# Reordered steps around the routing of an attention and mixture-of-experts block, with the residual kept divided by its gate and written into one of the two accumulators

## The reference

```
sa, ca, ga, sb, cb, gb = (silu(c) @ wmod) in six parts
ga, gb = sign * max(|g|, 0.25)
h = layernorm(x) * (1 + ca) + sa
r = h + recurrent_attention(h)
x = x + ga * (r + (silu(h2 @ Wgate) * (h2 @ Wval)) @ Wout)       # h2 = layernorm(r)
h = layernorm(x) * (1 + cb) + sb                                 # (2*512, 256)
p = softmax(h @ gate_weight.T)                                   # 16 experts, top 4 of each token
y = sum over the 4 of p_e * down_e(silu(gate_e h) * up_e h)      # 176 hidden
  + down_s(silu(gate_s h) * up_s h)                              # shared expert, 352 hidden
out = x + gb * y
```

## Time and profile before

| | |
|---|---|
| time, median of 3 runs | 368.24 us (368.22 to 368.97) |
| the profiled execution's own time | 365.12 us |
| its span, first to last instruction | 363.3 us |
| mean granted TensorE clock | 0.948 of full speed |
| PE busy | 317.4 us (87%) |
| DVE busy | 209.1 us (58%) |
| ACT busy | 176.0 us (48%) |
| POOL busy | 162.8 us (45%) |
| chain that ended last | PE 67%, DVE 15%, ACT 5%, DMA 5%, issue 4% |

### The profile page before, as it was taken

One profiled execution on the slowest core, in us unless ns is written; L12 is line 12 of the kernel. 1 busy time (PEld: TensorE's weight loads), 2 busy tenths in 40 slices (PEclk: granted clock), 3 DMA queues, 4 the chain that ended last, 5 costly groups with the idle time before them and its releaser, 6 DMA issues.

```text
span 363.3 us, 5639 instructions
## 1 busy us (share of the span) xinstructions
PE 317.4 (87%) x1424; PEld 236.1 (65%) x1424; DVE 209.1 (58%) x607; ACT 176.0 (48%) x338; POOL 162.8 (45%) x156
## 2 busy tenths in 40 slices
PE   6998989999999997999699787999999999999500
PEld 3785555766678876877497565777777777777300
DVE  4778998589576546594558834344343343343146
ACT  3488986798883533553271212443443444444200
POOL 3364487910001003256355571466566566666510
PEclk9889999999999999999988989999999999999855
DMA  6911031100019772002899464577766767765483
GB/s 206 359 68 59 1 115 59 60 0 0 2 48 361 158 144 73 2 17 98 231 321 325 150 204 157 111 111 108 121 113 105 115 118 109 120 113 62 56 231 133
DMA packets 43993, 44.91 MB, mean 124 GB/s; under 512 B 3387, under 2 KB 39995, under 8 KB 43963
## 3 DMA queue, kind: packets, MB, share of 16 engines
q1 hardware_dynamic: 35659, 33.66, 32.5%
q0 software_dynamic: 8304, 10.88, 18.7%
HBM read 27.74 MB, written 16.79 MB: 123 GB/s over the span
## 4 chain that ended last, share of the span: by engine, by line
PE 67%; DVE 15%; ACT 5%; DMA 5%; issue 4%; POOL 1%; SPq 1%; DVEq 0%; ACTq 0%; POOLq 0%
PE ps L1773 15%; PE ps L1800 10%; PE ps L1599 3%; PE ps L1361 3%; PE ps L1604 3%; PE ps L1600 3%; PE ps L1378 3%; PE ps L1362 3%; PE ps L1759 3%; PE ps L1786 3%; DMA acc_rows<-w,ids 2%; PE ps L1411 2%; PE ps L1418 1%; DVE w L1341 1%; DMA w<-in_wmod 1%
## 5 line engine op out<-in xcount | busy, mean ns | idle before, releaser
L546 POOL DMA_INDIRECT acc_rows<-w,ids x47 | 73.4, 1562 | 52.2 <-ACT w L866 49.6
L1773 PE MATMUL ps<-wup,w 128*128 x188 | 63.6, 460 | 1.5 <-DVE hm L1287 1.4
L1313 DVE TENSOR_TENSOR sg<-sg,ps 128x176 f32<-128x176 f32 x47 | 15.9, 338 | 68.4 <-ACT sg L858 68.4
L1800 PE MATMUL ps<-wdown,w 88*128 x188 | 48.6, 380 | 0.6 <-DVE w L1321 0.6
L533 POOL DMA_INDIRECT xs_rows<-h3x,slots x32 | 33.3, 1040 | 20.9 <-issue 20.9
L866 ACT ACTIVATE w<-ps,wv 128x256 f32<-128x256 f32 x47 | 22.3, 475 | 36.7 <-PE ps L1800 35.9
L1773 PEld LDWEIGHTS ps<-wup,w 128*128 128x128 f32 x188 | 32.0, 190 | 12.0 <-issue 1.9
L441 POOL TENSOR_TENSOR wsm_lo<-w,wsm_hi 128x512 fp32r<-128x512 f32 (+1 forms) x9 | 13.7, 1534 | 53.9 <-ACT wsm_hi L803 35.5
L1800 PEld LDWEIGHTS ps<-wdown,w 88*128 88x128 f32 x188 | 31.9, 190 | 3.8 <-issue 1.3
L858 ACT ACTIVATE sg<-ps 128x176 f32<-128x176 f32 x47 | 14.9, 317 | 33.3 <-PE ps L1773 33.3
L1599 PE MATMUL ps<-b_hi,wff_hi 128*128 128x512 f32 x64 | 26.9, 420 | 2.1 <-ACT w L756 1.3
(11 more groups left out here) (290 smaller groups left out, 705.9 us busy)
## 6 DMA issues: line engine op xcount, KB each, us to landing
xt<-xs_rows SPq DMA_DIRECT2D x47, 144.0 KB, 2.2
wup<-in_wmoe SPq DMA_DIRECT2D x4, 1408.0 KB
wdown<-in_wmoe SPq DMA_DIRECT2D x1, 2816.0 KB
xs_rows<-mod SPq DMA_DIRECT2D x17, 144.0 KB, 2.2
acc_rows<-mod SPq DMA_DIRECT2D x2, 1152.0 KB, 9.2
wdown<-in_wff SPq DMA_DIRECT2D x4, 512.0 KB, 6.4
w<-acc_rows SPq DMA_DIRECT2D x8, 256.0 KB, 4.6
w<-in_wsm SPq DMA_DIRECT2D x3, 512.0 KB, 9.2
```

Source lines behind the costliest of these rows:

```text
L546: nc.gpsimd.indirect_dma_start(acc_rows[n][:, :], bass.IndirectOffsetOnAxis(ids[:, i:i + 1], 0), ysb[i % YBUF], None, compute_op=ALU.add). ...
L1773: last = mm(bank(1, i)[:, 0:2 * FE].rearrange("p (w n) -> p w n", w=2), xT[i % 2][:, k * P:(k + 1) * P], up[:, k, :, bass.ds(e, FE)], star ...
L1800: last = mm(bank(3, i)[:, 0:C], hT[i % 2][:, h * P:(h + 1) * P], down[:, bass.ds(e + h * C, C)], start=h == 0, stop=h == 1)
```

## The change

Eight edits:

1. **PE.** `up.1.3` is split: its gate half comes first, then `logits.0` and `tx.0`, then its value half, then `rank.0` (before: `rank.0` came after `down.1.2` and `up.1.4`). `tm` waits for both halves of `acc` at once.
2. **ACT.** `ehigh.0`, `ehigh.1`, `ehigh.2` come earlier: behind `hid.0.5`, behind `h2.1.1` and behind `hid.1.1`. `exp.0` comes earlier, `h3hi.0` later. The second half of `acc.1` goes to DVE.
3. **DVE.** `lgsub.0`, `topk.0`, `rank.0` come earlier, `h3lo.0` later, `egated.0.0` ahead of `hn3.1`. New are `recip` (the reciprocal of the gate's rows of both sequences, 128x512), `over.0` and `over.1` (`hm` times the reciprocal, 128x1024 each) and `acc.1`.
4. **DVE, tables.** `early` is split into `ends` (what SP needs for the ends of the lists) and the rest, which comes after `elo.0.2`; `need` comes after `elo.1.1`; `late` leaves the text and is done in four pieces in the first four rounds of the tile loop.
5. **DVE and ACT, sums.** `sum` copies without the factor of the gate; `finish` thus leaves in `hm` the residual divided by the gate plus the shared expert.
6. **POOL.** `elow.1` comes ahead of `root.0.1`, and `scatter.0.2` ahead of `root.1.1`.
7. **SP.** The lists' ends are written in groups of four with their addresses read together, 12 of 16 ahead of the first tile loads. Behind the first four tile loads SP waits for `finish` of each sequence and stores `hm` (512 KB each) into accumulator 1. The second tile's addition waits for both stores.
8. **End.** For each quarter DVE adds the two accumulators and multiplies the sum by the gate's row: four sums and four products in place of eight of each.

```diff
-    down.0.4 t2.1 up.0.7 ... tm.0 rows up.1.2 down.1.0 down.1.1 t3.0 up.1.3
-    logits.0 tx.0 down.1.2 up.1.4 rank.0 down.1.3 up.1.5 ...
+    down.0.4 t2.1 up.0.7 ... tm.0 rows up.1.2 down.1.0 down.1.1 t3.0 ug.1.3
+    logits.0 tx.0 uv.1.3 rank.0 down.1.2 up.1.4 down.1.3 up.1.5 ...
@@ SCALAR_PLAN
-    silu.0.5 silu.0.6 hid.0.5 hid.0.6 h2hi.1.0 h2hi.1.1 silu.0.7 h2.1.0 h2.1.1 silu.1.0 hid.0.7 hid.1.0 acc.0 rows
-    silu.1.1 hid.1.1 ehigh.0 silu.1.2 hid.1.2 h3.0 silu.1.3 ehigh.1 tx.0 hid.1.3 silu.1.4 exp.0 h3hi.0 hid.1.4 ehigh.2
+    silu.0.5 silu.0.6 hid.0.5 ehigh.0 hid.0.6 h2hi.1.0 h2hi.1.1 silu.0.7 h2.1.0 h2.1.1 ehigh.1 silu.1.0 hid.0.7 hid.1.0
+    acc.0 rows silu.1.1 hid.1.1 ehigh.2 silu.1.2 hid.1.2 h3.0 silu.1.3 tx.0 exp.0 hid.1.3 silu.1.4 hid.1.4
+    silu.1.5 hid.1.5 h3hi.0 silu.1.6 ...
@@ VECTOR_PLAN
-    hn3.0 prod.1.2 h3.0 hidlo.1.2 prod.1.3 lgsub.0 hidlo.1.3 prod.1.4 topk.0 rank.0 h3lo.0 hidlo.1.4 pre.1
-    prod.1.5 hidlo.1.5 prod.1.6 hidlo.1.6 prod.1.7 hidlo.1.7 sum3.1 var3.1 hn3.1 egated.0.0 h3.1 egated.0.1
-    lgsub.1 elo.0.0 topk.1 rank.1 early elo.0.1 egated.0.2 h3lo.1 elo.0.2 need egated.1.0
-    late elo.1.0 egated.1.1 sum.0 finish.0 elo.1.1 egated.1.2 elo.1.2 sum.1 finish.1
+    hn3.0 prod.1.2 h3.0 hidlo.1.2 lgsub.0 prod.1.3 topk.0 rank.0 hidlo.1.3 prod.1.4 hidlo.1.4 pre.1
+    prod.1.5 hidlo.1.5 h3lo.0 recip prod.1.6 hidlo.1.6 over.0 prod.1.7 hidlo.1.7 acc.1 sum3.1 var3.1 egated.0.0 hn3.1 h3.1 egated.0.1
+    lgsub.1 elo.0.0 topk.1 rank.1 ends elo.0.1 egated.0.2 h3lo.1 elo.0.2 early egated.1.0
+    elo.1.0 over.1 egated.1.1 sum.0 finish.0 elo.1.1 need egated.1.2 elo.1.2 sum.1 finish.1
@@ POOL_PLAN
-    root.0.0 root.1.0 elow.0 root.0.1 elow.1 elow.2 scatter.0.0 scatter.0.1 root.1.1 scatter.0.2 scatter.0.3 ...
+    root.0.0 root.1.0 elow.0 elow.1 root.0.1 elow.2 scatter.0.0 scatter.0.1 scatter.0.2 root.1.1 scatter.0.3 ...
@@ SP
-            for e in range(NE // 2):
-                empty_end(e)
+            for e in range(0, NE - 4, 4):
+                empty_ends(e, e + 4)
             sp.wait_ge(s("tab_ready"), 2)
             sp.wait_ge(s("scattered"), 16 * (NB * NT - EARLY_T) * TOPK)
             for i in range(RING):
                 load_tile(i)
-            for e in range(NE // 2, NE):
-                empty_end(e)
-            for i in range(RING, EARLY):
+            sp.wait_ge(s("filled"), 16 * NACC)
+            for b in range(NB):
+                sp.wait_ge(s("tw_used"), 2 * NB + b + 1)
+                sp.dma_start(acc_rows[1][b * T:(b + 1) * T, :].rearrange("(t p) c -> p t c", p=P), hm[b][:, :, :]
+                             ).then_inc(s("filled"), 16)
+            for i in range(RING, RING + 2):
+                load_tile(i)
+            empty_ends(NE - 4, NE)
+            for i in range(RING + 2, EARLY):
                 load_tile(i)
@@ DVE, new steps
+            def recip():
+                dve.wait_ge(s("rows_sb"), 1)
+                dve.wait_ge(s("hn_ready"), 3)
+                at["recip"] = done(nc.vector.reciprocal(rgb, gbr[:, :, :]))
+            def over(b):
+                dve.wait_ge(s("hn2_ready"), NB + b + 1)
+                dve.wait_ge(s("dve_order"), at["recip"])
+                at["over", b] = done(nc.vector.tensor_tensor(hm[b][:, :, :], hm[b][:, :, :],
+                                     rgb[:, b, :].unsqueeze(1).broadcast_to([P, NT, C]), ALU.mult))
@@ DVE, the end
-            for k in range(NACC):
-                for b in range(NB):
-                    for h in range(2):
-                        ...
-                        link(nc.vector.tensor_tensor(given, given, gbr[...], ALU.mult))
-                        ...
-                        last = nc.vector.tensor_tensor(rows, rows, given, ALU.add)
+            for b in range(NB):
+                for h in range(2):
+                    first, last = (tok(W[b][k])[:, 2 * h:2 * h + 2, :] for k in range(NACC))
+                    rows = hm[b][:, 2 * h:2 * h + 2, :]
+                    for k in range(NACC):
+                        dve.wait_ge(*acc_in[(k * NB + b) * 2 + h])
+                    link(nc.vector.tensor_tensor(first, first, last, ALU.add))
+                    nc.vector.tensor_tensor(rows, first, gbr[...], ALU.mult).then_inc(s("y_ready"), 1)
```

More of the change, by code:

```diff
@@ L100 @@
     sqq.0 chunkhi.3 chunkhi.4 chunk.3 wsm.6 chunk.4 sqv.1 chunkhi.5 chunk.5 sqq.1 sqk.1
-    root.0.0 root.1.0 elow.0 root.0.1 elow.1 elow.2 scatter.0.0 scatter.0.1 root.1.1 scatter.0.2 scatter.0.3 scatter.1.0 scatter.1.1 scatter.1.2 scatter.1.3
+    root.0.0 root.1.0 elow.0 elow.1 root.0.1 elow.2 scatter.0.0 scatter.0.1 scatter.0.2 root.1.1 scatter.0.3 scatter.1.0 scatter.1.1 scatter.1.2 scatter.1.3
 """
@@ L380, in _, with empty_ends @@
             sp.wait_ge(s("tab_ready"), 1)
-            def empty_end(e):
-                row = nc.sync.value_load(ends[0:1, e:e + 1], min_val=1 + SPACE * e, max_val=1 + SPACE * e + CAP)
-                sp.dma_start(xs_rows[bass.ds(row, P), :], empty_rows).then_inc(s("emptied"), 16)
+            def empty_ends(lo, hi):
+                rows = [nc.sync.value_load(ends[0:1, e:e + 1], min_val=1 + SPACE * e, max_val=1 + SPACE * e + CAP)
+                        for e in range(lo, hi)]
+                for row in rows:
+                    sp.dma_start(xs_rows[bass.ds(row, P), :], empty_rows).then_inc(s("emptied"), 16)
             def load_tile(i):
@@ L768, in acc @@
                 act.wait_ge(s("modc_ready"), 2)
-                for c in range(KC):
+                for c in range(KC - b):
                     nc.scalar.activation(W[b][3][:, c, :], PB(b)[:, c, :], ACT.Copy,
@@ L1293, in _ @@
                 "o1": o1, "osig": osig, "sqe": sqe, "gated": gated, "outlo": outlo, "wo": wo, "var2": var2, "hn2": hn2, "h2lo": h2lo,
-                "prod": prod, "hidlo": hidlo, "pre": pre, "sum3": sum3, "var3": var3, "h3": h3, "hn3": hn3, "h3lo": h3lo, "lgsub": lgsub, "topk": topk,
-                "egated": moe_gated, "elo": moe_lo, "rank": rank, "early": early_table, "need": late_need_, "late": late_table, "sum": sum_out, "finish": finish,
+                "prod": prod, "hidlo": hidlo, "acc": acc, "recip": recip, "over": over, "pre": pre, "sum3": sum3, "var3": var3, "h3": h3, "hn3": hn3, "h3lo": h3lo, "lgsub": lgsub, "topk": topk,
+                "egated": moe_gated, "elo": moe_lo, "rank": rank, "ends": ends_, "early": early_table, "need": late_need_, "sum": sum_out, "finish": finish,
             }
@@ L1739, in _ @@
                 "ig": ig, "iglo": iglo, "ga": ga, "ssk": ssk, "og": og, "ssv": ssv, "u": u, "mem": mem, "oc": oc, "vo": vo, "wo": wo, "tw": tw, "t2": t2,
-                "up": ff_up, "down": ff_down, "tm": tm, "t3": t3, "logits": logits, "rank": rank, "rows": rows, "tx": tx, "st": sum_to_tokens,
+                "up": ff_up, "ug": ff_gate, "uv": ff_value, "down": ff_down, "tm": tm, "t3": t3, "logits": logits, "rank": rank, "rows": rows, "tx": tx, "st": sum_to_tokens,
                 "eg": moe_gate, "ev": moe_value, "edown": moe_down,
```

91 lines of the change are left out of this document (53 added, 38 removed).

## The result

The changed kernel took 372.61 us (median; 371.06 to 375.46), the kernel before 368.61 (368.22 to 369.79; three of its four runs are the ones known before): ratio 1.0156, 95% interval 1.0103 to 1.0208. The prediction, 365.4 us and faster, was wrong. The profiled execution took 371.56 us with a span of 369.8 us, 6.4 longer than before.

What follows compares the result with a forecast made beforehand. PE was taken to bound the tile loop and, with holes, the chain ahead of it; DVE works at the end. +1.65 + 1.25 - 3.95 - 1.75 = -2.8 us from 368.24 gives 365.4 us, range 361.2 to 368.3.

Steps and rivals of the forecast that it cites:

- `pre.0` beside `elow.1`: Ahead of `down.0.7`: POOL's `elow.1` holds up DVE's first `pre.0` operation, PE starts 1.65 us later; bounds 0 and 2.3.
- `elow.2` beside `hn3.0`: Ahead of `t3.0`: `elow.2` on POOL beside DVE's `hn3.0`, which reads one tensor and constants, costs 0.
- Reciprocal: On DVE ahead of `prod.1.6`: the 128x512 reciprocal takes 3.9 us; a cheap one, 0.69 us, was a rival with 0.22.
- the routing and the reciprocal: From `t3.0` to `down.1.7`: earlier routing gains 1.15 us, the reciprocal and `over.0` make PE wait; net +1.25 us.
- Fall of the clock: Rival, chance 0.11: logits, transposes, ranks and new holes lie closer; one stretch at 0.50 costs 1.65 us, giving 367.1 us.
- Tables: Shared expert's transposes: `late` leaves the path, PE's second group starts 2.33 us earlier, clock stays full; -3.95 us.
- Start of the loop: At the first tiles: starting the tile pipeline costs 0 to 0.5 us, given as bounds beside the tables' gain.
- End: Behind the tile loop: DVE's four pairs end at 359.0 against 360.75 us; -1.75 us, bounds -1.2 and -2.3.
- `root.1.1` held: Rival, chance 0.09: twelve scatters ahead of `root.1.1` on POOL delay it and all behind; up to +2.9 us, 371.1 us.
- what costs nothing: Split `acc.1`, `egated.0.0` ahead of `hn3.1`, `sum`'s copy, earlier scatters, SP's list ends and `hm` stores: no cost.
- The base: Profiled execution, 365.12 us, lies 3.1 below the median; the difference was taken over to the median, 368.24 us.

Runs made afterwards that it cites:

- the first two sets: First measurement of the changed kernel, 372.61 us; then its unedited repeat and three variants (list ends twice, weight splitting once), 368.91 to 371.05 us.
- e1_ends_single: Changed kernel with the list ends written one at a time, the last four too: 369.02 us, 1.0009 of the kernel before.
- k2: Changed kernel with the reciprocal moved from ahead of `prod.1.6` to between `prod.1.3` and `topk.0`: 363.23 us, 0.9890 of the kernel before.
- k1: Changed kernel, unedited, measured again on the chip of the second set: 364.22 us, 0.9873 of the kernel before.
- m1: Changed kernel, unedited, measured in the sixth and last set: 367.27 us, 0.9895 of the kernel before.
- h1: Kernel before with only the tables' change (`early`, `need`, `late` moved), SP's order as before: 364.62 us, 1.0020 of the kernel before.
- h2: Kernel before with only the end's edits, the reciprocal ahead of `sum3.1`, `over.0` and `over.1` ahead of `egated.0.1` and `egated.1.2`: 365.51 us, 1.0056.
- f3: Changed kernel with the tables as before, `early` right behind the ends and `late` whole ahead of `elo.1.0`: 371.41 us, 1.0127 of the kernel before.
- set 3: Changed kernel with `need` in the loop, ends behind later loads, or old tables; and tables plus end with old routing and splitting: 362.76, 380.19, 371.41, 360.98 us.
- after: First measurement and profile of the changed kernel, unedited: 372.61 us, 1.0156 of the kernel before.
- e2_split_back: Changed kernel with the weight splitting (`ehigh` on ACT, `elow` on POOL) back where the kernel before has it: 368.91 us, 1.0002 of the kernel before.

## Why the prediction was wrong, point by point

**What the first measurement held.** The stand, 5.89 of the 6.4 us of span; it put the time outside the forecast's range. The forecast had left PE's wait ahead of `edown.1.2` as it was, without a term and without a rival for it. It is 3.00 to 7.05 us in all five profiles of the first two sets and 0.78 in the fifteen others (fourteen of the later sets and the first one of before), with the unedited changed kernel on both sides (two with, three without) and one chip on both sides. It belongs to the moment and not to the list ends, `need`, the splitting or the chip alone. Whether the kernel before has it in such a moment was not seen: its only profiles are from moments without. Its medians rose there too, but less (368.5 against 366.5 us on one chip, the changed kernel 370.7 against 364.2). Nor is it shown how often the stand comes: `e1_ends_single` has the longest, 7.31 us, and a median only 0.55 above before's. What holds ACT and DVE while PE is idle stays open. One more thing marks the five traces. They hold 3,639 to 3,687 records of semaphore updates and the others 4,496 to 4,535, and the gap opens from 160 to 180 us on. So "remote" says little there: the record of the release may be among those missing. Whether the recording itself holds the engines in such a moment was not tried; in the stretches behind it the five cost what the others do (860 to 980: 0.79 to 1.08 us, against 0.81 to 1.06 in the unedited kernel without a stand).

**What is left without it.** The changed kernel's medians are 0.995, 0.994 and 0.9995 of before's, -0.2 to -2.3 us; forecast was -2.8. (Their ratios are 1.0016, 0.9873 and 0.9895; the kernel before had 0.9965 and 1.0037 against itself, so none of this is far from no change, and the 0.2% that I took for what a measurement tells was too little.) The terms, as means over the profiles:

- *`pre.0` beside `elow.1`, +1.65:* right, +1.65 in eleven of eleven profiles with that order and 0 in the nine others.
- *`elow.2` beside `hn3.0`, "0":* wrong, and of the terms of the sum this is the one that failed. I gave as reason that `hn3.0` reads one tensor and constants. It was shut out all the same, 2.86 us instead of 1.38. PE's wait before `t3.0` grows by 1.48, and mostly the clock falls behind it: in nine of the eleven profiles with this wait and in none of the nine with the shorter one. 520 to 680 costs 3.2 us in seven of the ten profiles with the reciprocal where the change has it and this order, 1.65 in the two without that fall, and 6.3 in the one with a long one. The Trainium skill (SBUF — State Buffer, Who interferes with whom) counts `tensor_scalar` among the operations that can take the pair of ports shared with GpSimd; I had used only its sentence on two inputs. The trace agrees with it by this row, though only the first of the four instructions is held.
- *Reciprocal, 3.9 us:* 3.34, so 6.5 ns an element; the dear end of my bounds was the right one. The Trainium skill's repeat count (VectorE: DVE Perf Modes, First, the fixed hardware budget) had given an estimate of 4.3; the measurement is lower. The holes were 0.44 and 0.81 and cost 1.1 us by `k2`, not 1.4 and 1.15. So the routing and the reciprocal, forecast at +1.25, cost only some +0.2: that is what is left of 1.65 without the 1.48. This error hid part of the one before.
- *Fall of the clock, a rival with 0.11:* far too small. "None fell from 134 to 172, with 3.5 us of holes" came from one execution. Of twelve profiles with the new routing order five have the long fall behind 183 us (+4.2 to +4.5), of the eight others one (+3.2); twenty are too few to say that the order makes it likelier. The Trainium skill (TensorE: Matmul & The Clock Gate, Part 1) says that one kernel has more or fewer slow products at its start, depending on the phase in which it starts. `k1` and `m1`, one kernel, differ in the same way later on (low from 186.3 to 199.9 and 203.3 to 206.8, or from 187.2 to 190.6 alone), but no run shows the phase.
- *Tables, -3.95:* -3.6 and -0.07, right in size and mechanism. SP's order, costed at nothing, was a condition of it by `h1`.
- *Start of the loop, 0 to 0.5:* +0.9. `h2` (the end's edits, old tables) shows 0.67 of it and `f3` 0.70, so the pieces of `late` cost some 0.2 to 0.3 and the rest comes with the end's edits; which of the stores or the longer queue was not tried.
- *End, -1.75:* mean -1.7 in the unedited changed kernel against the first trace, which has a short end (the other two of before are 1.2 and 0.85 longer), so -2.4 against the mean of the three: about the lower bound I had given.
- *`root.1.1` held (0.09):* did not happen; *what costs nothing* otherwise held.

Sum without the stand: 1.65 + 3.2 - 3.65 + 0.9 - 2.4 = -0.3 us, and -1.85 where the clock does not fall at 150 us; the medians say -0.2 to -2.3. That these lie inside the forecast's range is in part luck, as the errors of the terms offset each other. The range itself was not added up rightly: its two ends by the stated terms are 361.4 and 367.9 us, not 361.2 and 368.3.

**The base.** Up to 122 us, where no edit works, the profiles differ by -1.8 to +2.3 us, and from 680 to 780 by -3.1 to +4.5. I had taken the profiled execution's 3.1 us below the median as an offset to carry over. It belongs to that one execution: the two other profiles of before are 2.6 and 3.6 us longer, one by its start and its end (+1.5, +1.2), the other by the clock from 680 to 780 and its end (+3.2, +0.85).

## What to carry to other kernels

Before costing an operation of DVE beside one of GpSimd at nothing, look for a row where such a pair overlaps; "one input" was not enough. Where the clock can fall, one profile of before is one throw: ask for the waits ahead of each stretch, not for where it fell this time, and compare two traces by the start of the n-th product. When a wait appears that nothing in the profile ends, run the unedited kernel again elsewhere before explaining it: here each of the four variants of set 3 would have seemed to mend it. And a gain ahead of a loop arrives only if the loads of its first turns move with it.

## What the runs showed of the hardware

- A TENSOR_SCALAR of DVE with one large input in SBUF is held by a TENSOR_TENSOR of GpSimd: four of 128x256 took 2.86 us instead of 1.38, the first of them 1.89 instead of 0.41 (`after`, `e2_split_back`).
- A RECIPROCAL of 128x512 in f32 takes 3.34 us, one of 128x256 1.75, one of 128x4 0.18.
- In five profiles ACT or DVE took up PE's finished products late while PE was idle: PE's wait was 3.00 to 7.05 us, in the fifteen others 0.78. A fifth of the semaphore records is missing from those five; the cause is open.
- The same kernel ran the same 14 us around `t3.1` at 0.51 in one execution and at 0.88 in another.
